# Routing stage of a graph-attention and mixture-of-experts kernel, reordered: four parts per group instead of two, slot places by two products and a scan, expert weights turned at other points

## What is computed

```python
a = e_exp / e_sum[dst]
msg = feat_src[src] * a[:, :, None]
rst = segment_sum(msg, dst, num_segments=N)       # the edge loop leaves numerator and denominator in acc
x = x + rst.reshape(N, H * D)
flat = layernorm(x)
probs = softmax(flat @ router_w.T)                # 8 experts
topk_probs, topk_idx = top_k(probs, 2)
topk_probs = topk_probs / (sum(topk_probs) + 1e-09)
h1 = einsum('nc,ehc->neh', flat, w1);  h3 = einsum('nc,ehc->neh', flat, w3)
y = einsum('neh,ech->nec', silu(h1) * h3, w2)
out = x + einsum('ne,nec->nc', gates, y)          # gates: topk_probs at topk_idx, else 0
```

## Time and profile before

| | us |
|---|---|
| median of 3 runs | 4222.88 (4213.7 to 4223.18) |
| the profiled execution | 4178.57 |
| its span, first to last instruction | 4177.0 |
| its edge loop | some 288 to 2998 |
| its routing stage, with the barrier behind it | 2999.1 to 3248.9 |
| its expert stage | 3248.9 to 4177.0 |

### The profile page before, as it was taken

How to read it: one execution, slowest core, us unless ns; L and a number is a source line. 1 busy time by engine, 2 the same in 40 slices (tenths; PEclk the granted TensorE clock), 3 DMA queues, 4 the chain that set the end, 5 groups by cost and what they waited for, 6 DMA issues and landing times. The chain is left out here.

```text
span 4177.0 us, 59301 instructions
## 1 busy us (share of the span) xinstructions
PE 3178.8 (76%) x12650; PEld 2450.8 (59%) x12651; DVE 1978.3 (47%) x5334; ACT 1614.9 (39%) x3611; POOL 1857.7 (44%) x1906
## 2 busy tenths in 40 slices
PE   3532777777787777777777777777765899999997
PEld 1221666666666666666666666666554577777775
DVE  6730555555555555555555555555754122222221
ACT  2311544554444544544545444444432122222221
POOL 0005456666566665665666656566145111111111
PEclk9865667776667776677767767677755899999998
DMA  7734444444444444444444444446553312111113
GB/s 231 247 135 121 123 128 128 131 129 129 127 130 127 130 136 129 131 130 128 130 128 129 130 126 130 127 129 116 106 169 132 89 30 32 32 30 32 32 31 82
DMA packets 309415, 481.35 MB, mean 115 GB/s; under 512 B 161911, under 2 KB 237507, under 8 KB 300366
## 3 DMA queue, kind: packets, MB, share of 16 engines
q0 software_dynamic: 100848, 285.40, 27.9%
q1 hardware_dynamic: 206302, 192.99, 15.2%
q10 hardware_dynamic: 2000, 0.06, 0.0%
HBM read 408.52 MB, written 76.12 MB: 116 GB/s over the span
## 5 line engine op out<-in xcount | busy, mean ns | idle before, releaser
L809 POOL DMA_INDIRECT rows<-table,idx x1664 | 1574.3, 946 | 1089.9 <-issue 509.0
L852 PE MATMUL ps_acc<-rows,hot 128*128 128x264 f32 x3328 | 1315.2, 534 | 313.1 <-DVE acc L1140 229.2
L852 PEld LDWEIGHTS ps_acc<-rows,hot 128*128 128x128 f32 x3328 | 790.3, 262 | 455.5 <-issue 342.2
L1140 DVE TENSOR_TENSOR acc<-acc,ps_acc 128x264 f32 x832 | 356.3, 428 | 1004.2 <-PE ps_acc L852 523.6
L837 PEld LDWEIGHTS ps_term<-er,hot_t 128*128 128x128 f32 x3328 | 665.4, 259 | 239.4 <-issue 171.2
L837 PE MATMUL ps_term<-er,hot_t 128*128 x3328 | 618.9, 318 | 109.3 <-issue 57.1
L1126 DVE TENSOR_TENSOR rows<-rows,ps_p 128x512 f32<-128x512 f32 x832 | 566.0, 680 | 0.5 <-ACT ps_p L955 0.5
L944 ACT ACTIVATE hot<-iota_row,neg_rel 128x128 f32<-128x128 f32 x1664 | 545.4, 388 | 5.4 <-PE ps_acc L852 5.4
L1684 PE MATMUL ps_h<-w,acc 128*128 x1680 | 529.3, 458 | 0.5 <-ACT acc L1603 0.5
L1596 POOL DMA_INDIRECT x_dram<-acc,to x105 | 161.7, 1540 | 752.5 <-ACT acc L1612 752.5
L919 ACT COPY e_t<-ps_e 128x128 f32<-128x128 f32 x208 | 57.4, 276 | 961.3 <-remote 529.8
(11 more groups left out here) (262 smaller groups left out, 2955.5 us busy)
## 6 DMA issues: line engine op xcount, KB each, us to landing
dst_row<-rel_d SPq DMA_DIRECT2D x52, 1024.0 KB
rows<-table,idx POOLq DMA_INDIRECT x1664
rec<-rec_d SPq DMA_DIRECT2D x832, 24.0 KB
rec_d<-acc SPq DMA_DIRECT2D x16, 1050.0 KB
acc<-slots_x SPq DMA_DIRECT2D x105, 130.0 KB, 2.1
acc<-in_edge_attr_dram SPq DMA_DIRECT2D x16, 700.0 KB
wrow<-in_L_ffn_w_dram SPq DMA_DIRECT2D x16, 640.0 KB
table<-fo SPq DMA_DIRECT2D x49, 148.0 KB
```

The source lines that it names most:

```text
L809: pool.indirect_dma_start(rows[w][:, t, :], None, table, bass.IndirectOffsetOnAxis(ap=idx[w][:, t:t + 1], axis=0)).then_inc(gathered[w * Q ...
L852: last = pe.matmul(ps_acc[m % 2][:, 0:PW], hot[m // QI % 2][:, m % QI * G + j, :], rows[m // NI][:, tile_of(m % NI, j), 0:PW], start=(j == ...
L1140: dve.tensor_tensor(so_far, so_far, ps_acc[m % 2][:, 0:PW].rearrange("p (h d) -> p h d", h=HEADS), ALU.add).then_inc(added, 1)
```

## The change

The edge loop, the barrier behind it and the expert stage stay as they are. In the routing stage:

- `normal` is split into `sum_up` (division, sum, statistics) and `normal` (reciprocal root, normalized rows); `route` into `choose` (softmax, picks) and `send` (gates, slots). DVE runs `sum_up(0)`, `normal(0)`, `sum_up(1)` and then for each group `choose(g)`, `normal(g + 1)`, `send(g)`, `sum_up(g + 2)`. The denominators are inverted by group.
- The count within a group is taken by DVE in a scan along `[expert, block]` (`within`; `carry_on` sets it back to zero at each expert) to which the count of earlier groups is added (`so_far`, two buffers). PE then needs two products in place of eight: `ones` with `so_far`, and `not_above` (0 and -1) with the group's own picks `chosen`. `tally`, `added_to` and the wait on `tally_ok` are gone.
- PE turns 2 units ahead of group 0, one per group between the group's router products and its `places`, and the last 7 behind the last group. ACT's order is `copies(g)`, `exps(g)`, `root(g + 1)`, then the unit of the group.
- The matrices are loaded from ACT's queue, two transfers behind the copies of the unit whose buffer they take, and no longer from SP's.

```diff
-            def of_group(g):
-                return range(2 * EXPERTS * g // GROUPS, 2 * EXPERTS * (g + 1) // GROUPS)
+            FIRST_UNITS, UNITS = W_RING, 2 * EXPERTS
+            def unit_of(g):
+                return FIRST_UNITS + g
+            def last_units():
+                return range(unit_of(GROUPS), UNITS)
...
 def _(act):
+                        if n + W_RING < UNITS:
+                            load_weights(n + W_RING)
+                    for n in range(W_RING):
+                        load_weights(n)
                     root(0)
-                    copies(0)
-                    for n in of_group(0):
+                    for n in range(FIRST_UNITS):
                         keep_weights(n)
-                    for g in range(1, GROUPS):
-                        root(g)
-                        exps(g - 1)
+                    for g in range(GROUPS):
                         copies(g)
-                        for n in of_group(g):
-                            keep_weights(n)
-                    exps(GROUPS - 1)
+                        exps(g)
+                        if g + 1 < GROUPS:
+                            root(g + 1)
+                        keep_weights(unit_of(g))
+                    for n in last_units():
+                        keep_weights(n)
...
 def places(g):
-                            pe.wait_ge(tally_ok, g)
-                        pe.matmul(at, upper[:, :], hit[:, :, :], start=True, stop=False)
-                        for j in range(BC - 1):
-                            pe.matmul(at[:, j + 1:BC, :], ones[:, :], hit[:, j:j + 1, :].to_broadcast([P, BC - 1 - j, EXPERTS]), start=False, stop=False)
-                        pe.matmul(at, ones[:, :], tally[:, :].unsqueeze(1).to_broadcast(wide), start=False, stop=True).then_inc(slot_ps, 1)
+                        pe.matmul(at, not_above[:, :], chosen[:, :, :], start=True, stop=False)
+                        pe.matmul(at, ones[:, :], so_far[g % 2][:, :, :], start=False, stop=True).then_inc(slot_ps, 1)
...
+                    for n in range(FIRST_UNITS):
+                        turn_weights(n)
+                    for g in range(GROUPS):
+                        turn(g * BC)
+                        for b in range(g * BC, (g + 1) * BC):
+                            if b + 1 < (g + 1) * BC:
+                                turn(b + 1)
+                            logits(b)
+                        turn_weights(unit_of(g))
+                        places(g)
...
+                    for n in last_units():
+                        turn_weights(n)
...
 def choose(g):
+                            step(dve.tensor_tensor(by_expert, pick1[:, :, :], pick2[:, :, :], ALU.add))
+                        step(dve.tensor_tensor_scan(flat(within[:, :, :]), flat(carry_on[:, :, :]), flat(chosen[:, :, :]), 0.0, ALU.mult, ALU.add))
+                        before = so_far[(g - 1) % 2][:, :, BC - 1:BC] if g else none[:, :, :]
+                        dve.tensor_tensor(so_far[g % 2][:, :, :], within[:, :, :], before.to_broadcast([P, EXPERTS, BC]), ALU.add).then_inc(pick_ok, 1)
...
-                    for g in range(1, GROUPS):
-                        normal(g)
-                        route(g - 1)
-                    route(GROUPS - 1)
+                    sum_up(0)
+                    normal(0)
+                    sum_up(1)
+                    for g in range(GROUPS):
+                        choose(g)
+                        if g + 1 < GROUPS:
+                            normal(g + 1)
+                        send(g)
+                        if g + 2 < GROUPS:
+                            sum_up(g + 2)
```

More of the change, by code:

```diff
@@ L1204, in gnn_moe_kernel @@
             spare = sb(st, "spare", [P, 2, BC])
-            tally = sb(st, "tally", [P, EXPERTS])
-            added_to = sb(st, "added_to", [P, EXPERTS])
+            chosen = sb(st, "chosen", [P, EXPERTS, BC])
+            within = sb(st, "within", [P, EXPERTS, BC])
+            so_far = [sb(st, f"so_far{u}", [P, EXPERTS, BC]) for u in range(2)]
+            carry_on = sb(st, "carry_on", [P, EXPERTS, BC])
+            none = sb(st, "none", [P, EXPERTS, 1])
             slots_f = sb(st, "slots_f", [P, 2, BC])
             slots = sb(st, "slots", [P, 2, BLOCKS], I32)
-            upper = sb(st, "upper", [P, P])
+            not_above = sb(st, "not_above", [P, P])
             pad = sb(st, "pad", [P, RW])
@@ L1400, in turn_weights @@
                             last.then_inc(w_ps, 1)
-                    turn(0)
-                    for b in range(1, BLOCKS + 1):
-                        if b % BC:
-                            turn(b)
-                        logits(b - 1)
-                        if b % BC == BC - 1 and b > BC:
-                            places(b // BC - 1)
-                        if b % BC == 0:
-                            for n in of_group(b // BC - 1):
-                                turn_weights(n)
-                            if b < BLOCKS:
-                                turn(b)
-                    places(GROUPS - 1)
-                    pe.wait_ge(tally_ok, GROUPS)
+                    for n in range(FIRST_UNITS):
[8 more added lines that the diff above has]
+                        places(g)
                     pe.wait_ge(slot_used, GROUPS)
-                    pe.matmul(ps_s[:, 0:EXPERTS], ones[:, :], tally[:, :], start=True, stop=True).then_inc(count_ps, 1)
+                    pe.matmul(ps_s[:, 0:EXPERTS], ones[:, :], so_far[(GROUPS - 1) % 2][:, :, BC - 1], start=True, stop=True).then_inc(count_ps, 1)
+                    for n in last_units():
+                        turn_weights(n)
                 @block.vector
@@ L1439, in normal @@
                         join_stats(dve, step, stats, mv, tmp, var_ok, g + 1)
+                    def normal(g):
+                        r = g % RING
                         dve.wait_ge(std_ok, g + 1)
```

59 lines of the change are left out of this document (27 added, 32 removed).

## The result

The changed kernel takes **4192.06 us**, the median of four runs (4187.58 to 4198.93), beside 4220.23 for the kernel before (four runs now, 4213.7 to 4223.18; the table above had three of them): a ratio of 0.9937, 95% interval 0.9916 to 0.9958. It is 28 us faster. The prediction said 63, and its range ended at 4177, so it was wrong in size, though not in sign.

A forecast was written before the change was run, and what follows sets the result against it. Routing stage bound by a loop DVE, PE, DVE, ACT, DVE; after the change by POOL: 135.8 us of transfers to 3174.1, plus 11.4, starts the experts 63.4 us earlier. 4222.9 - 63.4 = 4160 us, range 4147 to 4177.

The forecast's parts named there:

- The work per group, 17.6 us: Routing stage, DVE: its own changed work sums to 17.6 us per group in place of a 29.5 us turn.
- The waits for places and root are covered: Routing stage, DVE: places and the root are ready before DVE asks, by margins of 2.2 and 2.7 us.
- The head: Start of routing stage: group 0's rows land in 6.5 us, choose starts at 3028.5, first POOL transfer at 3038.3.
- The step to 3018.6: Head of the stage, PE: free for group 0 about 3.6 copies later, at 3018.6, then 8.9 us for it.
- POOL runs through, to 3174.1: Routing stage, POOL: 98 transfers with 97 gaps of 0.30 us take 135.8 us without starving, from 3038.3.
- PE's chain of c + 15.1 us: Routing stage: PE finishes the next group 15.1 us after choose starts (c), ahead of DVE at 17.6 us.
- Collisions: POOL transfers beside DVE's 2.02 us steps: 2.3 us more per pair, five of seven pairs left in POOL's run.
- Seven units: Stage's end: the last seven weight units start at 3141.5, last copy at 3178.3 to 3181.1, ahead of POOL.
- The gain, 63.4 us: Whole routing stage: the expert stage begins at 3185.5, 63.4 us earlier than before.
- POOL starves: Rival, chance 0.12: DVE's turn exceeds 20.5 us; at 22 us the stage ends 7.3 us later, 4167 us.
- The slower rival: Rival, chance 0.03: DVE without pauses holds each POOL transfer to 2.53 us, stage 78 us later than before, 4301 us.

The follow-up runs named there:

- e11: The changed kernel, unedited, run again where the kernel before took 3618.5 us: 3569.8 us, ratio 0.9864, routing stage 185.3 us.
- e2: The changed kernel with the matrix loads issued on SP again: 4129.1 us, ratio 0.9900 to the kernel before at 4167.6 us.
- e14: The kernel before, unedited, run again for its trace: 3617.7 us beside 3618.5, ratio 0.9998, routing stage 234.9 us.
- e18: The changed kernel, unedited, run again: 4187.9 us, ratio 0.9923 to the kernel before at 4215.4 us.
- e15: The changed kernel with the old places (nine products, tally, added_to), so the new order alone: 4180.2 us, ratio 0.9924 to the kernel before.
- e17: The changed kernel with no units ahead of group 0, two per group, and a memset ahead of every second scatter: 4159.5 us, ratio 0.9861 to before.
- e16: The changed kernel with no units ahead of group 0, two per group, two at the end, no memsets: 4166.3 us, ratio 0.9898 to before.
- e3: The changed kernel with one short POOL memset ahead of every second scatter of the routing stage: 4119.9 us, ratio 0.9885 to before at 4167.6.
- e7: The changed kernel with a short POOL memset ahead of every second scatter and every second edge-loop gather: 4135.2 us, ratio 0.9806 to before.
- e6: The changed kernel with a short POOL memset ahead of every second scatter and every fourth edge-loop gather: 4166.7 us, ratio 0.9876 to before.
- e8: The kernel before with a short POOL memset ahead of every second gather and every second scatter: 3872.4 us, ratio 1.0688 to before at 3622.1.

## Why the prediction was wrong, point by point

- **The work per group, 17.6 us: right.** The first three turns of e11 are 17.64 to 17.67 us. The later ones, 17.9, 18.4 and 15.0, were not in the forecast: there DVE waits 11.1 us for router products in two groups and 0.8 us for a `row` buffer, which costs nothing, as POOL is the bound.
- **The waits for places and root are covered: right**, by the rows above. The waits for `ps_s` have no row, in the changed kernel as in e11.
- **The head: right in its sum.** First transfer 39.2 us into the stage forecast, 39.6 measured, 39.2 in e11. But its landing was not: the sum that needs `xg` starts 7.6 us into the stage, behind a wait for the transfer, where I had taken 6.5 us (in e2, whose loads all go by SP's queue, 5.3). The changed kernel, then e2:

```profile
3044.67 2.02 DVE L1438 TENSOR_TENSOR xg<-xg,acc 128x1792 f32<-128x1792 f32 x1 [3.21 <-DMA xg<-in_x_dram]
```
```profile
2992.87 2.03 DVE L1447 TENSOR_TENSOR xg<-xg,acc 128x1792 f32<-128x1792 f32 x1 [0.92 <-DMA xg<-in_x_dram]
```

  The Trainium skill (DMA: Bandwidth & Descriptors, section Issuing engines are not separate DMA queues) says that transfers of all issuing engines interleave on the same DMA engines; by these rows the trace agrees, as `xg` came 2.3 us later beside the matrices. The head is shorter than e2's all the same, its first `exps` 30.2 us into the stage beside 31.6. The step to 3018.6 in the working is 7.3 us, three distances of 2.44 between half units and not the 3.6 it names. So part of this agreement is luck.
- **POOL runs through from 38.3 on: the step that failed.** "So POOL runs through, to 3174.1" stood on PE's chain of c + 15.1 us, and that on durations of 8.9 us for the router products, taken from group 0, where POOL had not yet begun. Beside a long row of scatters the turns and products of one group took up to 30.5 (3186.4 to 3216.9, group 6). In e11 the whole step holds: 98 transfers in 135.3 us (105.8 busy and 29.5 between) against 135.8, no gap above 0.31, the last down 174.5 us into the stage against 175.0, the load 10.9 us later against 11.4. So the arithmetic was right, and a resource was missing from it: how late a signal comes.
- **Collisions: right.** Ten long transfers in e11 and eleven in the changed kernel, 1.65 to 2.68 us, all but one in pairs beside the two 2.02 us steps of DVE. The Trainium skill (SBUF — State Buffer, section Who interferes with whom) infers that writing descriptors is not held by `tensor_tensor`. By these rows POOL's instruction for an indirect transfer is held, which is what the forecast took from the earlier trace rows; whether the writing of descriptors or the reading of the slots is held, they do not tell.
- **Seven units: right in length, wrong in place.** From PE's first half to the last copy they took 36.8 us (3225.4 to 3262.3), forecast 36.8 (3141.5 to 3178.3). They began 188 us into the stage in place of 142, behind a last group that was 46 us late, and so became the end of the stage. In e11 the last copy ends 178 us into it, forecast 179 to 182.
- **The gain, 63.4 us: the baseline was mis-sized too.** I took the 50.3 us for `ps_s` as the kernel's own. By e14 about 15 us of before's stage are late signals. Without them the change is worth 49, and a forecast from e14's rows would have said so. With them it is 28 (e18: 27.5): the change made POOL's rows twice as long, and its stage is 40 us longer than in e11.
- **Rivals.** POOL starves, at 0.12 and 4167 us, was nearest by name. Its price was taken from waits of 2 us and not of 17. The slower rival had the right suspicion, that DVE and POOL without pauses disturb something, but looked for it in POOL's own transfers, whose mean fell from 1089 to 1068 ns.

Open is what makes a signal late. In the routing stage the rows say that it goes with POOL's indirect transfers and, beside each other, with their rate, and not with the bytes moved. In the edge loop a slower rate did not make it less. Under other conditions the same kernels have none of it, and what differs between the conditions was not tested; the records of e11 to e14 and of e15 to e18 even name the same chip number. Whether the limit is in descriptors, in completions or in what records them, no run here tells apart.

## What to carry to other kernels

Look for waits on inputs that were long done ("remote" here) before a forecast, and at what runs beside them: a duration read where a neighbour is idle holds only there. A change that takes the pauses out of one engine's row takes away what the others recovered in; a small pace in that row gave back 7 to 9 us where signals were late (e17 beside e16; e3 beside e2, whose loads go by another queue) and cost 14 us where none was. So time a pace under more than one condition: in the edge loop the memsets of e7 were worth 0.7 to 0.8% in one (e7 beside e6 and e3) and cost nearly 7% in the other (e8).

## What was not expected of the hardware

- Engines stood up to 13.0 us for signals whose work was done, beside rows of indirect transfers, from 13 to 17 us into the row (changed kernel, e15) to 2 to 4 us behind its end, at one transfer per 1.37 and 1.44 us. At 1.50 us (e3) there was none in the routing stage, at 1.52 (e6, e7, e17) 10 to 22 us of waits late in the row. POOL's own transfers stayed at 0.96 us all the while, but for the pairs beside DVE's long steps.
- The same unedited kernel took 4215 to 4223 us, 4167.6 us or 3618 to 3622 us by median. The difference stands almost wholly in the edge loop (2998 against 2453 us), with late signals all through it and a granted clock of 0.70 in the one and none and 0.80 in the other.
- A memset of 0.33 us between two transfers, with a wait behind it, lengthened their distance by only 0.3 us and not by the 0.47 expected.
